# A Perceiver block on one core: the cross attention's opening takes its PSUM banks in turn, and the key-bias constant is made ahead of the second half of turned Wk

## The chip, the cores and the metric

The kernel runs on one core of a Trainium2 chip. The metric is the device time of one execution in microseconds (us). TensorE is PE in the profile, its weight loads are PEld, VectorE is DVE, ScalarE is ACT, GpSimd is POOL and SyncE, which issues the loads here, is SP.

## The reference, cut to what matters

A transformer block of three parts: cross attention of 64 x 64 rows of x on 64 contexts of 256 rows, self attention, and a mixture of experts. The change is in the first.

```python
def _L0_xattn_ref(query, key, value, Wq, bq, Wk, bk, Wv, bv, Wo, bo, ln_gamma, ln_beta):
    q = (query @ Wq + bq).reshape(b, sq, N_HEAD, KEY_DIM)         # 16 heads of 64
    k = (key @ Wk + bk).reshape(b, key.shape[1], N_HEAD, KEY_DIM)
    v = (value @ Wv + bv).reshape(b, value.shape[1], N_HEAD, VALUE_DIM)
    scores = jnp.einsum('bqhd,bkhd->bhqk', q, k) / TEMP
    attn = jax.nn.softmax(scores, axis=-1)
    out = jnp.einsum('bhqk,bkhd->bqhd', attn, v).reshape(b, sq, N_HEAD * VALUE_DIM)
    out = out @ Wo + bo + residual
    ...
x = x + _L0_xattn_ref(_layernorm(x, axis=-1), ctx_1024, ctx_1024, ...)
x = x + _L0_attn_ref(_layernorm(x, axis=-1), ...)
x = x + _L0_ffn_ref(_layernorm(x, axis=-1), ...)
```

## The kernel before

**Work.** Cross attention goes over the 64 batches in 16 groups of four. The keys are not projected. Instead each head's q is multiplied with its turned Wk (`do_fold`, one "fold" for each of eight heads of a half), and the result `qk` meets the transposed context `ctxT` in the scores. Every fp32 operand is split into an upper part, written by ACT out of PSUM (`ctxT_hi`, `qk_hi`, `wk_hi`), and a lower part, written by DVE as the PSUM value less the upper (`ctxT_lo`, `qk_lo`, `wk_lo`, L653). A product is then three matmuls (`exact3`, L930) or two (L973). So every result in PSUM goes PE, ACT, DVE, and only after DVE is its bank free.

**Steps.** A group has eight steps s: half = s // 4 picks the heads, b = s % 4 the batch. A step's chain is `do_scores` (24 matmuls into one of two score buffers), `peaks` on DVE (a maximum over the scores L690, then `top` L693 and `nbias` L695, which also read `qbk`), `exps` on ACT (L562), the division by the sum (`normalise`, on DVE in steps 0 and 7, on POOL in steps 1 to 6), and in the next step the transposes of the probabilities (`do_pT`, L1003, eight of them in two banks) and `do_pc` (with the context). scores(s), peaks(s), exps(s) and pT(s) stand below for these in step s of group 0; pT(1) is made of the probabilities of scores(0).

**The opening.** What comes before the loop is written as group -1 (first q for heads 0 to 7, their folds and all four `ctxT`) and group 0, which besides its own work turns the second half of Wk (`do_wkT`, L918, four pieces "wk") in steps 0 and 1 and makes the key-bias constant `qbk0` in step 0. The constant is q times bk for each row and head: POOL multiplies Wq by bk and adds up over each head (`weights_by_bk`, L460 and L466, result `wqb`), PE multiplies the normalised x by `wqb` (`do_qbk`, 12 small matmuls), and DVE keeps it (`keep_qbk`, L714). peaks(0) needs it. POOL then splits the contexts of group 0 (`split_ctx`, L437 and L439), which only `do_pc` reads.

**Banks.** Four PSUM banks are a ring (`ring`) for everything but the scores. Which item uses which bank is a table: `PAIR_BANKS` and `SINGLE_BANKS`, read by `ring_bank`. `ring_order` lists the items in the order in which they are used. `bank_for` lets PE wait until DVE or ACT has freed the item that had the bank before; semaphores `freed0` to `freed3` count this. The table is the same for every group. In group -1 it gives: xT 3, q 1 and 2, ctxT(0) 1, folds 0 to 7 the banks 1, 3, 0, 1, 2, 0, 3, 2, and ctxT(1) to ctxT(3) all bank 2. In group 0 it gives wk 0 to 3 the banks 0 to 3 and qbk0 bank 2; pT(1) uses banks 2 and 3.

**Order.** Every engine runs its instructions in the order in which its function (`tensor`, `vector`, `scalar`, `gpsimd`, `sync`) writes them. No scheduler moves anything.

Of the kernel before, what the change touches and what calls it, by code (L numbers as in the profile page):

```python
# [19 lines left out]
ALU = mybir.AluOpType  # L20
# [4 lines left out]
DC = D // P  # L25
# [5 lines left out]
DK = 64  # L31
# [9 lines left out]
RING = 4  # L41
# [77 lines left out]
def ring_order(kind):  # L119
# [10 lines left out]
    for s in range(STEPS):  # L130
        half, b = divmod(s, GB)
        if kind == 0 and s < 2:
            out += [("wk", 2 * s), ("wk", 2 * s + 1)]
        if kind == 0 and s == 0:
            out.append(("qbk0",))
        if half == 1 and g.next:
# [32 lines left out]
}  # L169
SINGLE_BANKS = {"ctxT": (1, 2, 2, 2), "o": (3, 0), "wk": (0, 1, 2, 3), "xT": (3,), "qbk": (1,), "qbk0": (2,)}  # L170


def ring_bank(key):

    if key[:2] in PAIR_BANKS and len(key) == 3:
        return PAIR_BANKS[key[:2]][key[2]]
    return SINGLE_BANKS[key[0]][key[1] if len(key) > 1 else 0]


def cross_attention(nc, ctx, t, x1_dram, ident, early, late, scores_banks, ring, following):  # L180
# [100 lines left out]

    bank_turns = [Turns(lambda kind, k=k: [key for key in ring_order(kind) if ring_bank(key) == k], -1, GROUPS)
                  for k in range(RING)]
# [5 lines left out]
    def place(g, key, groups_on=0):  # L289


        k = ring_bank(key)
        if isinstance(g.at, int):
            c, f = bank_turns[k].index(g.at + groups_on, key)
        else:
            c, f = bank_turns[k].index(g.at, key)
            c += bank_turns[k].loop * groups_on
        return k, (c + 1, f)
# [120 lines left out]
    def gpsimd(pool):  # L419
# [37 lines left out]

        def weights_by_bk(c):

            nc.gpsimd.tensor_tensor(products[:, 0], wq_raw[:, c, :], biases[:, 0], ALU.mult).then_inc(wqb_step, 1)  # L460
            pool.wait_ge(wqb_step, WQB_STEPS * c + 1)
            n = DK // 2
            parts = products[:, 0].rearrange("p (h d) -> p h d", d=DK)
            for i in range(WQB_STEPS - 1):
                out = parts[:, :, 0:n] if n > 1 else wqb[:, c, :].unsqueeze(2)
                nc.gpsimd.tensor_tensor(out, parts[:, :, 0:n], parts[:, :, n:2 * n], ALU.add).then_inc(wqb_step, 1)  # L466
                pool.wait_ge(wqb_step, WQB_STEPS * c + i + 2)
                n //= 2

        for g in turns(pool):  # L470
            if g.kind == -1:
                rsqrt(g, 0, ln_stats, ln_rstd, 1)
                pool.wait_ge(wq_in[0], 16)
                pool.wait_ge(wq_in[1], 16)
                pool.wait_ge(bk_in, 16)
                for c in range(DC):
                    weights_by_bk(c)
                nc.gpsimd.tensor_copy(wqb_hi[:, :, :], wqb[:, 0:DC, :]).then_inc(wqb_step, 1)
                pool.wait_ge(wqb_step, WQB_STEPS * DC + 1)
                nc.gpsimd.tensor_tensor(wqb_lo[:, :, :], wqb[:, 0:DC, :], wqb_hi[:, :, :],  # L480
# [153 lines left out]
    def vector(dve):  # L634
# [143 lines left out]
        for g in turns(dve):  # L778
# [40 lines left out]
            for s in range(STEPS):  # L819
                half, b = divmod(s, GB)  # L820
                if s == 0 and g.kind == 0:

                    for i in range(2):
                        wk_lower(g, i)
                    dve.wait_ge(wqb_done, 1)
# [6 lines left out]
                if g.cur:  # L832
                    peaks(g, s)
                if g.kind == 0 and s == 1:
                    for i in range(2, 4):
                        wk_lower(g, i)
# [74 lines left out]
    def tensor(pe):  # L911
# [161 lines left out]
        for g in turns(pe):  # L1073
# [1640 lines left out]
```

## Time and profile before

| | |
|---|---|
| three runs | 2158.69, 2160.35, 2160.77 us; median 2160.35 us |
| the profiled execution | 2161.38 us, of which its span is 2159.6 us |
| PE busy | 2099.8 us (97% of the span) |
| DVE, ACT, POOL busy | 1568.7 us (73%), 1269.5 us (59%), 941.1 us (44%) |
| mean granted clock of TensorE | 0.991 of full speed |
| share of PE in the chain that ended last | 75% |

The profiled execution is 1.03 us over the median, and what lies outside its span is 1.78 us. The views used below are: the chain of work that ended last, in order of time; the timeline, engine by engine; busy time and granted clock by stretch; and the issues of the loads with their time to landing. A bracket at the end of a timeline row gives the idle time of the engine before it and what ended it.

### The profile page before, as it was taken

To read this page: it belongs to the slowest core of one execution; us is meant where nothing else is said; L and a number is where in the kernel's file an instruction comes from. 1 tells how busy PE (TensorE), PEld (TensorE's weight loads), DVE (VectorE), ACT (ScalarE), POOL (GpSimd) and SP (SyncE) were. 2 spreads that over 40 slices of the span, in tenths; PEclk is the share of its full clock that TensorE was granted. 3 is DMA by queue.
4 is the path that set the end of the run, shared out by engine and by line. 5 is a ranking of instruction groups with operands and counts; after the bars stand their busy time and mean duration, and the time that the engine had idled before them with its cause. 6 is when DMAs were issued, how large, how long until landed. Compare 5 with 4: busy or idle time off the path is not lost.

```text
span 2159.6 us, 46904 instructions
## 1 busy us (share of the span) xinstructions
PE 2099.8 (97%) x15864; PEld 1853.6 (86%) x15865; DVE 1568.7 (73%) x2774; ACT 1269.5 (59%) x3067; POOL 941.1 (44%) x786
## 2 busy tenths in 40 slices
PE   7999999999999999999999999899998999999997
PEld 6889899888988898898998888678886888888886
DVE  5667767777677677677677776699996877666665
ACT  4656666665666666556666656467775335555553
POOL 3322332333233224223323332278884334777775
PEclk9999999999999999999999999999999999999999
DMA  5000010010000000100100100145442222333332
GB/s 154 6 25 22 13 34 19 15 34 15 19 24 24 19 24 10 34 22 12 34 19 15 34 10 1 48 157 167 156 129 94 88 79 55 56 53 53 53 54 42
DMA packets 100685, 103.90 MB, mean 48 GB/s; under 512 B 11952, under 2 KB 90160, under 8 KB 100624
## 3 DMA queue, kind: packets, MB, share of 16 engines
q1 hardware_dynamic: 86992, 84.47, 12.5%
q0 software_dynamic: 13632, 18.62, 5.4%
q8 instruction: 37, 0.61, 0.1%
q14 instruction: 24, 0.20, 0.0%
HBM read 72.52 MB, written 30.54 MB: 48 GB/s over the span
## 4 chain that ended last, share of the span: by engine, by line
PE 75%; POOL 9%; issue 6%; DVE 5%; ACT 2%; DMA 2%; POOLq 0%; SPq 0%; DVEq 0%; ACTq 0%
PE banks L930 38%; PE banks L973 6%; PE banks L1003 5%; PE banks L1031 5%; PE banks L1018 5%; POOL out_dram L2431 4%; PE banks L1672 3%; POOL r_x L2395 3%; PE banks L2270 2%; POOL index L2402 2%; DMA out_dram<-r_y,index 1%; PE banks L960 1%; PE banks L1735 1%; PE banks L1694 1%; PE banks L1751 1%
## 5 line engine op out<-in xcount | busy, mean ns | idle before, releaser
L930 PE MATMUL banks<-ctxT_hi,qk_hi 128*128 128x256 f32 x1024 | 301.5, 294 | 0.0
L930 PE MATMUL banks<-ctxT_hi,qk_lo 128*128 128x256 f32 x1024 | 290.1, 283 | 0.0
L930 PE MATMUL banks<-ctxT_lo,qk_hi 128*128 128x256 f32 x1024 | 288.2, 281 | 0.0
L562 ACT ACTIVATE probs<-banks,nbias 128x256 f32<-128x256 f32 x512 | 236.3, 486 | 81.1 <-DVE nbias L695 80.7
L451 POOL TENSOR_TENSOR rinv<-rsum,inverse 128x4 f32<-128x4 f32 x96 | 96.7, 1007 | 410.9 <-ACT probs L562 410.9
L569 ACT ACTIVATE pc<-banks 128x512 f32<-128x512 f32 x256 | 153.0, 598 | 190.4 <-PE banks L930 187.2
L653 DVE TENSOR_TENSOR qk_lo<-banks,qk_hi 128x512 fp32r<-128x512 f32 x256 | 163.7, 686 | 88.4 <-ACT qk_hi L524 88.3
L690 DVE TENSOR_REDUCE peak<-banks 128x4 f32<-128x1024 f32 x128 | 156.4, 1222 | 81.6 <-PE banks L930 81.6
L653 DVE TENSOR_TENSOR pT_lo<-banks,pT_hi 128x512 fp32r<-128x512 f32 x256 | 164.7, 685 | 58.2 <-ACT pT_hi L524 57.7
L930 PE MATMUL banks<-pT_hi,ctx_hi 128*128 128x512 f32 x512 | 204.7, 400 | 1.7 <-DVE pT_lo L653 1.7
L930 PE MATMUL banks<-pT_hi,ctx_lo 128*128 128x512 f32 x512 | 201.6, 394 | 0.0
L930 PE MATMUL banks<-pT_lo,ctx_hi 128*128 128x512 f32 x512 | 200.8, 392 | 0.0
L930 PEld LDWEIGHTS banks<-ctxT_lo,qk_hi 128*128 128x128 f32 x1024 | 196.1, 191 | 0.0
L930 PEld LDWEIGHTS banks<-ctxT_hi,qk_hi 128*128 128x128 f32 x1024 | 194.1, 190 | 0.6
L930 PEld LDWEIGHTS banks<-ctxT_hi,qk_lo 128*128 128x128 f32 x1024 | 193.0, 188 | 0.0
L454 POOL TENSOR_TENSOR probs<-probs,rinv 128x1024 f32<-128x1024 f32 x96 | 181.8, 1893 | 17.5 <-POOL rinv L451 17.5
L524 ACT ACTIVATE qk_hi<-banks 128x512 fp32r<-128x512 f32 x256 | 137.6, 601 | 77.8 <-PE banks L973 77.7
L437 POOL CAST ctx_hi<-ctx_raw 128x512 fp32r<-128x512 f32 x64 | 39.0, 610 | 299.6 <-PE banks L930 287.4
L673 DVE SCALAR_TENSOR_TENSOR q_st<-banks,bq_low,q_st 64x256 fp32r<-64x256 f32 x256 | 112.5, 479 | 55.3 <-ACT q_st L546 53.3
L1003 PE MATMUL banks<-ident,probs 128*128 128x128 f32 x1024 | 136.0, 275 | 7.3 <-DVE wk_lo L653 3.3
L524 ACT ACTIVATE pT_hi<-banks 128x512 fp32r<-128x512 f32 x256 | 139.8, 601 | 5.0 <-PE banks L1003 3.9
L973 PE MATMUL banks<-q_st,wk_hi 128*128 128x256 f32 x512 | 135.7, 299 | 5.5 <-DVE ctxT_lo L653 3.1
(271 smaller groups left out, 6161.0 us busy)
## 6 DMA issues: line engine op xcount, KB each, us to landing
ctx_raw<-in_ctx_dram SPq DMA_DIRECT2D x64, 256.0 KB, 2.7
experts_w<-in_L_ffn_We_dram SPq DMA_DIRECT2D x24, 512.0 KB, 3.9
x_in<-in_x_dram SPq DMA_DIRECT2D x16, 256.0 KB, 2.8
x_again<-in_x_dram SPq DMA_DIRECT2D x16, 256.0 KB, 2.8
x_stream<-z SPq DMA_DIRECT2D x16, 256.0 KB, 2.1
s_x<-x_stream SPq DMA_DIRECT2D x32, 128.0 KB, 3.7
s_x_again<-x_stream SPq DMA_DIRECT2D x32, 128.0 KB, 3.2
x_normalised<-s_xl SPq DMA_DIRECT2D x32, 128.0 KB, 1.7
```

Source lines behind the costliest of these rows:

```text
L454: nc.gpsimd.tensor_tensor(probs[:, s % 2], probs[:, s % 2], rinv[:, s % 2, :].unsqueeze(2).broadcast_to([P, PAIRS, SK]), ALU.mult).then_in ...
L524: nc.scalar.activation(out, bank, ACT.Identity).then_inc(hi_done, 1)
L562: nc.scalar.activation(probs[:, s % 2, p, :], scores[:, s % 2, p // 2, (p % 2) * SK:(p % 2 + 1) * SK], ACT.Exp, bias=nbias[:, s % 2, p:p + ...
L569: nc.scalar.activation(pc[:, c, :, at], bank.rearrange("p (h q) -> p h q", h=HALF), ACT.Identity).then_inc(free, 1)
L653: nc.vector.tensor_tensor(out, rows(ring[:, k, :]), hi, ALU.subtract).then_inc(freed[k], 1)
L673: last = nc.vector.scalar_tensor_tensor(out=q_st[DK:P, h, :], in0=ring[DK * hp:DK * hp + DK, k, i * GT:(i + 1) * GT], scalar=bq_low[:, tar ...
L690: link(nc.vector.tensor_reduce(peak[:, s % 2, :], scores[:, s % 2, :, :].rearrange("p j (i k) -> p (j i) k", i=2), AX_X, ALU.max))
L930: last = nc.tensor.matmul(out, a, b, start=(n == 0), stop=(n == 3 * len(pairs) - 1))
L973: last = nc.tensor.matmul(bank[:, c * GT:(c + 1) * GT], w[:, target * HALF + h, c * P:(c + 1) * P], q_st[:, h, :], start=(n == 0), stop=(n ...
L1003: last = nc.tensor.transpose(bank[:, p * P:(p + 1) * P], probs[:, (s - 1) % 2, p, k * P:(k + 1) * P], ident[:, :])
L1018: last = nc.tensor.matmul(bank[hp * DK:(hp + 1) * DK, i * GT:(i + 1) * GT], wv[:, c, col:col + DK], pc[:, c, h, :], start=(c == 0), stop=( ...
L1031: last = nc.tensor.matmul(bank[:, n * D:(n + 1) * D], oT[:, m, n * P:(n + 1) * P], wo[:, m, :], start=(m == first), stop=(m == first + PAI ...
```

## The change

1. In group -1 the bank of an item is its place in `ring_order`, modulo 4: xT 0, q 1 and 2, ctxT(0) 3, folds 0 to 7 the banks 0, 1, 2, 3, 0, 1, 2, 3, and ctxT(1), (2), (3) the banks 0, 1, 2. All other groups keep the table.
2. In group 0, wk 0 to 3 take the banks 0, 1, 0, 1 and qbk0 takes bank 3.
3. In step 0 PE does `do_qbk` ahead of `do_wkT` 0 and 1, and DVE does `keep_qbk` and `peaks` ahead of `wk_lower` 0 and 1.
4. POOL makes `wqb` in two halves of the heads, the first of which waits only for the first half of Wq: four chunks of 512 columns where there were two of 1024, each of seven operations.

```diff
     for s in range(STEPS):
         half, b = divmod(s, GB)
+        if kind == 0 and s == 0:
+            out.append(("qbk0",))
         if kind == 0 and s < 2:
             out += [("wk", 2 * s), ("wk", 2 * s + 1)]
-        if kind == 0 and s == 0:
-            out.append(("qbk0",))
...
-SINGLE_BANKS = {"ctxT": (1, 2, 2, 2), "o": (3, 0), "wk": (0, 1, 2, 3), "xT": (3,), "qbk": (1,), "qbk0": (2,)}
+SINGLE_BANKS = {"ctxT": (1, 2, 2, 2), "o": (3, 0), "wk": (0, 1, 0, 1), "xT": (3,), "qbk": (1,), "qbk0": (3,)}
-def ring_bank(key):
+def ring_bank(key, kind):
+    if kind == -1:
+        return ring_order(kind).index(key) % RING
...
-        def weights_by_bk(c):
-            nc.gpsimd.tensor_tensor(products[:, 0], wq_raw[:, c, :], biases[:, 0], ALU.mult).then_inc(wqb_step, 1)
+        def weights_by_bk(half, c):
+            done = WQB_STEPS * (DC * half + c)
+            cols = slice(half * HALF * DK, (half + 1) * HALF * DK)
+            nc.gpsimd.tensor_tensor(products[:, 0, cols], wq_raw[:, c, cols], biases[:, 0, cols],
+                                    ALU.mult).then_inc(wqb_step, 1)
...
-                pool.wait_ge(wq_in[0], 16)
-                pool.wait_ge(wq_in[1], 16)
                 pool.wait_ge(bk_in, 16)
-                for c in range(DC):
-                    weights_by_bk(c)
+                for half in range(2):
+                    pool.wait_ge(wq_in[half], 16)
+                    for c in range(DC):
+                        weights_by_bk(half, c)
...
                 if s == 0 and g.kind == 0:
-                    for i in range(2):
-                        wk_lower(g, i)
                     dve.wait_ge(wqb_done, 1)
                     keep_qbk(g, ("qbk0",))
...
                 if g.cur:
                     peaks(g, s)
-                if g.kind == 0 and s == 1:
-                    for i in range(2, 4):
+                if g.kind == 0 and s < 2:
+                    for i in range(2 * s, 2 * s + 2):
                         wk_lower(g, i)
...
                 if g.cur:
                     do_scores(g, s)
+                if g.kind == 0 and s == 0:
+                    pe.wait_ge(wqb_done, 1)
+                    do_qbk(g, ("qbk0",))
                 if g.kind == 0 and s < 2:
                     for i in range(2 * s, 2 * s + 2):
                         do_wkT(g, i)
-                if g.kind == 0 and s == 0:
-                    pe.wait_ge(wqb_done, 1)
-                    do_qbk(g, ("qbk0",))
```

**PE in group -1**, before: the first matmul of ctxT(0), of fold 0, 4, 5 and 7, and the three ctxT after the folds, with the semaphores that each waits for (in the rows, `banks` is PSUM and `pc` the room in which the raw weights lie).

```order
L960 MATMUL banks<-ident,ctx_raw 128x128 [waits freed1,ctx_in0]
L973 MATMUL banks<-q_st,wk_hi 128x256 [waits freed1,setup_lo]
L973 MATMUL banks<-q_st,wk_hi 128x256 [waits freed2,setup_lo]
L973 MATMUL banks<-q_st,wk_hi 128x256 [waits freed0]
L973 MATMUL banks<-q_st,wk_hi 128x256 [waits freed2]
L960 MATMUL banks<-ident,ctx_raw 128x128 [waits freed2,ctx_in1]
L960 MATMUL banks<-ident,ctx_raw 128x128 [waits freed2,ctx_in2]
L960 MATMUL banks<-ident,ctx_raw 128x128 [waits freed2,ctx_in3]
```

The same matmuls in the changed kernel:

```order
L963 MATMUL banks<-ident,ctx_raw 128x128 [waits ctx_in0]
L976 MATMUL banks<-q_st,wk_hi 128x256 [waits freed1,setup_lo]
L976 MATMUL banks<-q_st,wk_hi 128x256 [waits freed0,setup_lo]
L976 MATMUL banks<-q_st,wk_hi 128x256 [waits freed1]
L976 MATMUL banks<-q_st,wk_hi 128x256 [waits freed3]
L963 MATMUL banks<-ident,ctx_raw 128x128 [waits freed0,ctx_in1]
L963 MATMUL banks<-ident,ctx_raw 128x128 [waits freed1,ctx_in2]
L963 MATMUL banks<-ident,ctx_raw 128x128 [waits freed2,ctx_in3]
```

ctxT(0) no longer waits for a bank. Fold 0 waited on bank 1 for ctxT(0) itself, and now waits on bank 1 only for the first q. The last three ctxT wait on three banks instead of on one.

**DVE in step 0 of group 0**, before, from the lower part of Wq's second half on:

```order
L647 TENSOR_TENSOR wq_lo<-pc,wq_hi 128x2x512 [waits wq_hi_done]
L653 TENSOR_TENSOR wk_lo<-banks,wk_hi 128x512 [waits hi_done] x2
L714 SCALAR_TENSOR_TENSOR qbk<-banks,wqb 64x2x8 [waits filled2,wqb_done]
L690 TENSOR_REDUCE peak<-banks 128x4 [waits scores_done,small_in,freed2]
L693 SCALAR_TENSOR_TENSOR top<-peak,qbk 128x4 [waits dve_step]
L695 TENSOR_TENSOR nbias<-qbk,top 128x4 [waits dve_step]
L725 RECIPROCAL rinv<-rsum 128x4 [waits exp_done]
```

The same in the changed kernel:

```order
L652 TENSOR_TENSOR wq_lo<-pc,wq_hi 128x2x512 [waits wq_hi_done]
L719 SCALAR_TENSOR_TENSOR qbk<-banks,wqb 64x2x8 [waits filled3,wqb_done]
L695 TENSOR_REDUCE peak<-banks 128x4 [waits scores_done,small_in,freed3]
L698 SCALAR_TENSOR_TENSOR top<-peak,qbk 128x4 [waits dve_step]
L700 TENSOR_TENSOR nbias<-qbk,top 128x4 [waits dve_step]
L658 TENSOR_TENSOR wk_lo<-banks,wk_hi 128x512 [waits hi_done] x2
L730 RECIPROCAL rinv<-rsum 128x4 [waits exp_done]
```

The two `wk_lo` moved from ahead of the constant to behind `nbias`, which ACT waits for.

**PE in steps 0 and 1 of group 0**, before: wk 0 and 1 (their first transposes), the constant, wk 2 and 3, and pT(1) in its two banks.

```order
L918 MATMUL banks<-ident,pc 64x128 [waits wk_in1]
L930 MATMUL banks<-wqb_hi,xT_hi 128x16 [waits freed2,wqb_done]
L918 MATMUL banks<-ident,pc 64x128 [waits freed2,wk_in1]
L1003 MATMUL banks<-ident,probs 128x128 [waits freed2,probs_done]
L1003 MATMUL banks<-ident,probs 128x128 [waits freed3]
```

The same in the changed kernel, where the constant comes first:

```order
L933 MATMUL banks<-wqb_hi,xT_hi 128x16 [waits wqb_done]
L921 MATMUL banks<-ident,pc 64x128 [waits freed0,wk_in1]
L921 MATMUL banks<-ident,pc 64x128 [waits freed1,wk_in1]
L1006 MATMUL banks<-ident,probs 128x128 [waits freed2,probs_done]
L1006 MATMUL banks<-ident,probs 128x128 [waits freed3]
```

Before, pT(1) waited in banks 2 and 3 for the `wk_lo` of wk 2 and 3; now those banks were last used by ctxT(3) and by the constant, and it is wk 2 and 3 that wait, for wk 0 and 1.

## Rows read from the trace of the kernel before

**Rows 1.** By stretch: length, busy PE, PEld, DVE, ACT, POOL, clock, DMA share, GB/s.

```profile
80.00:1100.00 1020.00, 1018.67 (x7190) 912.46 (x7190) 739.17 (x1346) 626.45 (x1661) 320.10 (x267) 1.00 0.07 22
```

**Rows 2.** Chain that ended last, in order of time: start, us, what.

```profile
21.16 3.58 PE banks L973 x16
...
34.33 4.77 PE banks L930 x24
...
39.10 1.90 PE banks L918 x32
...
41.00 1.45 PE banks L930 x12
...
51.80 2.89 PE banks L930 x24
```

**Rows 3.** Timeline of PE: start, us, what, then idle before and releaser.

```profile
31.11 0.63 PE L960 MATMUL banks<-ident,ctx_raw 128*128 128x128 f32 x4 [1.50 <-DVE ctxT_lo L653]
...
33.98 0.56 PE L930 MATMUL banks<-ctxT_hi,qk_hi 128*128 128x256 f32 x1
...
50.64 1.16 PE L1003 MATMUL banks<-ident,probs 128*128 128x128 f32 x8 [3.34 <-DVE wk_lo L653]
```

**Rows 4.** Timeline of DVE and ACT in the folds.

```profile
15.52 3.58 DVE L673 SCALAR_TENSOR_TENSOR q_st<-banks,bq_low,q_st 64x256 fp32r<-64x256 f32 x8
...
20.33 0.68 DVE L653 TENSOR_TENSOR ctxT_lo<-banks,ctxT_hi 128x512 fp32r<-128x512 f32 x1
...
24.76 2.31 ACT L524 ACTIVATE qk_hi<-banks 128x512 fp32r<-128x512 f32 x4 [0.33 <-PE banks L973]
...
25.39 2.51 DVE L653 TENSOR_TENSOR qk_lo<-banks,qk_hi 128x512 fp32r<-128x512 f32 x4 [0.24 <-ACT qk_hi L524]
```

**Rows 5.** By stretch, PE alone: length, busy (matmuls), granted clock, DMA share, GB/s.

```profile
22.00:23.00 1.00, 1.00 (x7) 0.50 0.97 389
```

**Rows 6.** Timeline of DVE and ACT from the constant to the second wk_lo.

```profile
42.55 0.73 DVE L714 SCALAR_TENSOR_TENSOR qbk<-banks,wqb 64x16 f32<-64x16 f32 x4 [0.18 <-PE banks L930]
...
43.31 1.23 DVE L690 TENSOR_REDUCE peak<-banks 128x4 f32<-128x1024 f32 x1
...
44.97 0.47 ACT L562 ACTIVATE probs<-banks,nbias 128x256 f32<-128x256 f32 x1 [3.32 <-DVE nbias L695]
...
47.14 1.22 DVE L726 TENSOR_TENSOR probs<-probs,rinv 128x1024 f32<-128x1024 f32 x1
...
49.81 1.28 DVE L653 TENSOR_TENSOR wk_lo<-banks,wk_hi 128x512 fp32r<-128x512 f32 x2
```

**Rows 7.** Timeline of POOL: products of wqb, its end, last context split.

```profile
14.03 2.43 POOL L460 TENSOR_TENSOR probs<-pc,oT 128x1024 f32<-128x1024 f32 x1 [8.19 <-DMA pc<-in_L_xattn_Wq_dram]
...
26.68 0.25 POOL L480 TENSOR_TENSOR wqb_lo<-wqb,wqb_hi 128x32 fp32r<-128x32 f32 x1
...
33.27 1.27 POOL L439 TENSOR_TENSOR ctx_lo<-ctx_raw,ctx_hi 128x512 fp32r<-128x512 f32 x1
```

**Rows 8.** Issues of two loads on SP's queue, and their time to landing in us.

```profile
2.32 0.47 SPq L370 DMA_DIRECT2D oT<-in_L_xattn_bk_dram  x1
...
17.00 0.53 SPq L389 DMA_DIRECT2D wo<-in_L_xattn_Wo_dram  x1
...
oT<-in_L_xattn_bk_dram SPq DMA_DIRECT2D x1, 512.0 KB, 7.3
...
wo<-in_L_xattn_Wo_dram SPq DMA_DIRECT2D x1, 1024.0 KB, 11.9
```

**Rows 9.** Timelines of POOL and DVE where the two meet.

```profile
55.65 1.89 POOL L454 TENSOR_TENSOR probs<-probs,rinv 128x1024 f32<-128x1024 f32 x1 [0.18 <-POOL rinv L451]
...
55.97 1.59 DVE L693 SCALAR_TENSOR_TENSOR top<-peak,qbk 128x4 f32<-128x4 f32 x1
...
141.02 0.61 POOL L437 CAST ctx_hi<-ctx_raw 128x512 fp32r<-128x512 f32 x1
...
141.13 0.52 DVE L695 TENSOR_TENSOR nbias<-qbk,top 128x4 f32<-128x4 f32 x1
```

More of the change, by code:

```diff
@@ L280, in cross_attention @@
     pool_past = sem("pool_past")
-    bank_turns = [Turns(lambda kind, k=k: [key for key in ring_order(kind) if ring_bank(key) == k], -1, GROUPS)
+    bank_turns = [Turns(lambda kind, k=k: [key for key in ring_order(kind) if ring_bank(key, kind) == k], -1, GROUPS)
                   for k in range(RING)]
@@ L289, in place @@
     def place(g, key, groups_on=0):
-        k = ring_bank(key)
+        k = ring_bank(key, g.at + groups_on if isinstance(g.at, int) else g.kind)
         if isinstance(g.at, int):
@@ L456, in normalise @@
                                     ALU.mult).then_inc(probs_pool, 1)
-        def weights_by_bk(c):
-            nc.gpsimd.tensor_tensor(products[:, 0], wq_raw[:, c, :], biases[:, 0], ALU.mult).then_inc(wqb_step, 1)
-            pool.wait_ge(wqb_step, WQB_STEPS * c + 1)
+        def weights_by_bk(half, c):
[3 more added lines that the diff above has]
+                                    ALU.mult).then_inc(wqb_step, 1)
+            pool.wait_ge(wqb_step, done + 1)
             n = DK // 2
-            parts = products[:, 0].rearrange("p (h d) -> p h d", d=DK)
+            parts = products[:, 0, cols].rearrange("p (h d) -> p h d", d=DK)
             for i in range(WQB_STEPS - 1):
-                out = parts[:, :, 0:n] if n > 1 else wqb[:, c, :].unsqueeze(2)
+                out = parts[:, :, 0:n] if n > 1 else wqb[:, c, half * HALF:(half + 1) * HALF].unsqueeze(2)
                 nc.gpsimd.tensor_tensor(out, parts[:, :, 0:n], parts[:, :, n:2 * n], ALU.add).then_inc(wqb_step, 1)
-                pool.wait_ge(wqb_step, WQB_STEPS * c + i + 2)
+                pool.wait_ge(wqb_step, done + i + 2)
                 n //= 2
@@ L472, in gpsimd @@
                 rsqrt(g, 0, ln_stats, ln_rstd, 1)
-                pool.wait_ge(wq_in[0], 16)
-                pool.wait_ge(wq_in[1], 16)
                 pool.wait_ge(bk_in, 16)
-                for c in range(DC):
-                    weights_by_bk(c)
+                for half in range(2):
+                    pool.wait_ge(wq_in[half], 16)
+                    for c in range(DC):
+                        weights_by_bk(half, c)
                 nc.gpsimd.tensor_copy(wqb_hi[:, :, :], wqb[:, 0:DC, :]).then_inc(wqb_step, 1)
-                pool.wait_ge(wqb_step, WQB_STEPS * DC + 1)
+                pool.wait_ge(wqb_step, WQB_STEPS * DC * 2 + 1)
                 nc.gpsimd.tensor_tensor(wqb_lo[:, :, :], wqb[:, 0:DC, :], wqb_hi[:, :, :],
```

## The prediction

> **What bounds the kernel now.** First read the share of PE in the chain that ended last, in the small table: 75%. Then the busy time by stretch [rows 1]: from 80 to 1100 us PE is busy for 1018.67 of 1020 us at the full clock. Once the loop runs there is no gap that could swallow or return time, and the change leaves every instruction of the loop and every bank in it alone. So the change is worth what it moves the start of the loop, one for one, and all of it has to be read in the first 62 us.
>
> There the chain in order of time [rows 2] and the timelines [rows 3, 4, 6] show four things to look for.
>
> (a) PE starts fold 0 at 21.16 us, right after DVE's ctxT_lo of 20.33 [rows 2, 4], since ctxT(0) had fold 0's bank.
>
> (b) After the folds, ctxT(1) to ctxT(3) go through one bank. Each has to be made by PE, split by ACT, lowered by DVE, and only then comes the next: PE starts one at 31.11 us after 1.50 us of idling for DVE's ctxT_lo of the one before it [rows 3]. scores(0) starts only at 33.98.
>
> (c) PE, which had idled, runs at half clock: the 24 matmuls of scores(0) cost 4.77 us on the chain and the 24 of scores(2) 2.89 [rows 2]. The stretch 22 to 23 us has a granted clock of 0.50, that is 1.2 of 2.4 GHz, after PE's idle time up to 21.16 [rows 2, 5].
>
> (d) From the end of scores(0), 39.10, the exps(0) on ACT are waited for until 44.97, and pT(1) comes at 50.64, after 3.34 us of idling, released by wk_lo [rows 2, 3, 6].
>
> **Banks in turn, group -1.** No instruction is added or removed. ctxT(0) finds bank 3 empty, so it follows the turned Wk at once, and fold 0 waits only for the first four heads of q: DVE is half through its 3.58 us of q_st at 15.52 + 1.8 = 17.3 [rows 4]. Folds 0 to 3 then fit in four banks. From fold 4 on a bank is needed again, and DVE is what frees it: it ends ctxT_lo at 20.33 + 0.68 = 21.0 as before, and then finds four results waiting. It lowers one every 0.63 us (four in 2.51), ACT's four take 2.31, so DVE sets the pace [rows 4]. Fold 6's lower half is then done at 21.0 + 7 x 0.63 = 25.4, which frees bank 2 for ctxT(3); with its 0.63 us on PE [rows 3] scores(0) starts at **26.0 instead of 33.98: 8.0 us**. The three ctxT_lo lie behind the folds on DVE and end near 27.8; only scores(1) and later need them.
>
> **The clock in scores(0).** In my replay PE has folds and transposes from 21.8 to 26 with gaps of under half a microsecond, while before it had 1.50 us of idling ahead of each ctxT. I take the full clock, 2.89 instead of 4.77 us. scores(0) then ends at 26.0 + 3.0 = **29.0 instead of 39.10: 10.1 us by now**. Bounds: nothing (clock as before, 1.9 us lost), or the full clock; the value next to it is scores(2).
>
> **The constant first.** Before, wk 0 and 1 (1.90 us) and the 12 small matmuls (1.45) lay between scores(0) and DVE's qbk [rows 2]; now only the 1.45. From the end of the constant on PE, 42.45, to the exps(0), 44.97, are 2.52 us: qbk 0.73, the maximum 1.23, top, nbias [rows 6]. So exps(0) could start at 29.0 + 1.45 + 2.5 = 33.0. On ACT wk_hi 0 and 1 stand ahead of it: PE ends wk 1 at 30.45 + 1.90 = 32.4, and at 0.6 us for one upper half ACT is free at 33.0 too. That edit gains 1.9 us and has no more to give.
>
> **What peaks(0) now meets.** At 26 to 34 us POOL works. Rows show what that does: POOL's operation from 55.65 took 1.89, and DVE's top of 128x4, started at 55.97, took 1.59, up to POOL's end; a nbias started at 141.13 took 0.52 under a CAST that had started at 141.02 and ran 0.61 [rows 9]. top and nbias read SBUF twice. The maximum, qbk and the lower halves read PSUM. POOL's last context split ended at 33.27 + 1.27 = 34.5 before [rows 7], ten microseconds before peaks(0). Now top comes at 29.0 + 1.45 + 0.1 + 0.73 + 1.23 = 32.5. POOL starts its products when bk has landed, 2.32 + 7.3 = 9.6 [rows 8], not at 14.03; before, the stretch took 26.93 - 14.03 = 12.9 us [rows 7], and it now has 14 operations more at 0.15 to 0.3 us of fixed cost each (a tiny one takes 0.25), about 3.5. wqb is ready at 26 to 27 (needed on PE at 29.0, so hidden by 2 us; before it was ready 14 us early, so this edit gains nothing), and the splits, 7.6 us, end at 33.7 to 35. So top and nbias each can wait for an operation of 0.61 or 1.27 us: 0 to 2.5 us in all, and I take **1.2**: exps(0) at 34.2.
>
> The Trainium skill, page "SBUF — State Buffer", section "Who interferes with whom", puts it as a rule: a DVE instruction with two SBUF inputs and a GpSimd instruction that reads SBUF exclude each other, and whoever issues second is fully blocked. By that rule, which the rows above agree with, the wait in peaks(0) is a part of the sum and not an accident. Without it the sum would be 0.4 us better, as the next part shows.
>
> **From exps(0) to pT(1).** wk_lo 0 and 1 (1.28) moved behind nbias; exps(0) hide them (2.17 us until the multiplication starts). Probabilities are ready 2.17 + 1.22 = 3.4 us after exps(0) start [rows 6], at 37.6. PE has by then done, without a gap: 29.0 + 1.45 + 1.90 (wk 0, 1) + 2.89 (scores(1)) + 1.90 (wk 2, 3, whose banks wk_lo 0 and 1 free at 34.9 and 35.6) = 37.2. So pT(1) comes at 37.6, and at 37.2 if the ports cost nothing: the first 0.8 us of a port wait cost 0.4. Before, pT(1) also waited for DVE's maximum over scores(1) and wk_lo, 48.36 to 50.5; now banks 2 and 3 are long free. **50.64 becomes 37.6: 13.0 us.** Behind it nothing is later by more: nbias(1) is ready 1.45 us after the multiplication [rows 6], at 39.1, as ACT ends pT_hi; scores(2), q and pc follow pT(1) as before. The end of the group, the loads for group 1 (issued before 40 us, read after 68) and the loop shift along.
>
> **Sum.** 2161.38 - 13.0 = 2148.4 for an execution like the profiled one, which lay 1.03 over the median: **2147.4 us**.
>
> **Rivals.**
> 1. *The clock stays low in scores(0), or falls in the folds.* PE does idle from about 19.4 to 21.8, and an idle stretch of 3 us had brought the half clock at 21 [rows 2, 5]. scores(0) costs 1.9 more, the folds up to 0.7: 2149.3 to 2150.0.
> 2. *The port costs more.* DVE's product of the two biases (two SBUF inputs, at 13.0, two operations ahead of the q_st of 15.52) now stands against POOL, which began only at 14.03. One POOL operation ahead of it is up to 1.27 us (a split's) and goes straight into q_st and the folds; with the full 2.5 us in peaks(0), of which 1.7 pass: 3.0 instead of the 0.4 that the sum has, 2150.0.
> 3. *A better turn in step 2.* In peaks(2) top lost 1.4 us to POOL [rows 9]. If the exps(1) end only 0.4 us later against scores(2) than they did, top and nbias get ahead of POOL: 2146.0.
> 4. *Slower: DVE finds no gap at all.* If the biases' product doesn't get in between two POOL operations, it waits until POOL's first pause, after the splits, at 33.7 or later instead of 13.0. All of DVE's queue, q_st first, is 20.7 us late, less 13.0: 2168.0. It decides from 26.0 on. Against it: nbias at 141.13 ended at 141.65, between POOL's CAST and its next operation [rows 9].
> 5. *The gain is eaten by something that doesn't shift.* peaks(0) also wait for the small loads, the last of which, wo, lands at 17.00 + 11.9 = 28.9 [rows 8]; needed at 31.3, so 2.4 us are in hand, and each later microsecond costs one. Or the new order doesn't show at all, because another wait had been just behind the banks. Half eaten would be 2154, all of it 2160.
>
> **Numbers.** Forecast 0.62, rival 1 0.16, rival 2 0.08, rival 3 0.06, rival 4 0.03, rival 5 0.05 (0.02 half, 0.03 more). The range reaches from rival 3 less the spread of the runs to rivals 1 and 2 and a microsecond: 2144.8 to 2151.2, and leaves out 0.12 or so with the edges. A measurement can tell 0.2%, 4.3 us, from no change: faster 0.93 (all but 4 and most of 5), the same 0.03, slower 0.04.
>
> **What the profile after would show.** scores(0) starts near 26.0, and its 24 matmuls take 2.9 us at clock 1.00 (rival 1: 4.8 at 0.50); no PE idling for ctxT_lo ahead of ctxT(2) and (3) over 0.5 us; exps(0) at 33 to 34.3, with top or nbias longer than 0.2 us and ending with a POOL operation (rival 2: the biases' product over 1.3 us); pT(1) at 37.2 to 37.6, released by the probabilities; wqb_lo done by 27; and from 62 us on the old trace, 13 us earlier. Wrong it would be if scores(0) starts after 28, if the biases' product lasts past 15, or if steps 1 to 4 of group 0 are longer than before by more than a microsecond.

## The result, and the profile after

The changed kernel takes 2147.5 us (median of four runs, 2144.19 to 2149.09), the one before 2160.56 (2158.69 to 2161.27). The ratio is 0.9938, with a 95% interval of 0.9926 to 0.995: 13.1 us faster. 2147.4 was forecast, in a range of 2144.8 to 2151.2. The profiled execution took 2147.61 us, its span is 2145.9, so 13.7 less than the span before.

The page of the changed kernel, its span and the row of TensorE. PE is busy for as long as before within 2.7 us, so that of the 13.7 us that the span lost about 11 are idle time of PE.

```profile
span 2145.9 us, 46808 instructions
...
PE 2097.1 (98%) x15864; PEld 1850.5 (86%) x15865; DVE 1568.1 (73%) x2774; ACT 1271.4 (59%) x3067; POOL 946.7 (44%) x800
```

The chain that ended last, over the stretch that changed (start, us, what):

```profile
20.07 0.61 DVE ctxT_lo L658
...
20.73 4.33 PE banks L976 x20
...
25.06 1.39 PE banks L963 x12
...
26.45 4.12 PE banks L933 x36
...
30.56 1.90 PE banks L921 x32
...
35.53 1.90 PE banks L921 x32
...
37.42 1.02 PE banks L1006 x8
...
41.36 1.24 DVE peak L695
...
42.62 1.65 DVE top L698
```

From 20.73 to 41.3 us the chain is PE alone (the pieces left out are PE's too): 20 matmuls of the folds, the twelve transposes of the last three contexts in one go (1.39 us where the profile before had 2.13 us for each four, [rows 3]), scores(0) with the constant (4.12 us for 36 matmuls), wk, scores(1), wk, pT(1), scores(2). The waits of DVE, of ACT and of DVE and POOL for each other are off it. Then peaks(2) comes with top at 1.65 us, as before [rows 9].

PE's timeline at the starts of scores(0) and pT(1), which answer to [rows 3], and the busy time with the granted clock for two stretches (stretch, length, PE busy, clock, DMA share, GB/s), which answer to [rows 5]:

```profile
26.20 0.36 PE L933 MATMUL banks<-ctxT_hi,qk_hi 128*128 128x256 f32 x1
...
37.36 1.09 PE L1006 MATMUL banks<-ident,probs 128*128 128x128 f32 x8
...
22.00:24.00 2.00, 2.00 (x11) 0.50 1.04 391
...
27.00:28.00 1.00, 1.00 (x11) 1.00 0.06 19
```

scores(0) starts at 26.20 (before 33.98) at the full clock, pT(1) at 37.36 (before 50.64) and without a wait. In the folds the clock was at half, 1.2 of 2.4 GHz.

DVE, ACT and POOL around peaks(0), which answer to [rows 6, 7]:

```profile
31.44 1.22 DVE L695 TENSOR_REDUCE peak<-banks 128x4 f32<-128x1024 f32 x1
...
32.70 0.28 DVE L698 SCALAR_TENSOR_TENSOR top<-peak,qbk 128x4 f32<-128x4 f32 x1
...
33.02 0.52 DVE L700 TENSOR_TENSOR nbias<-qbk,top 128x4 f32<-128x4 f32 x1
...
33.57 0.47 ACT L567 ACTIVATE probs<-banks,nbias 128x256 f32<-128x256 f32 x1 [0.46 <-DVE nbias L700]
...
31.68 1.28 POOL L441 TENSOR_TENSOR ctx_lo<-ctx_raw,ctx_hi 128x512 fp32r<-128x512 f32 x1
...
32.91 0.61 POOL L439 CAST ctx_hi<-ctx_raw 128x512 fp32r<-128x512 f32 x1
```

top ran until 32.98, when POOL's ctx_lo ended at 32.96, and nbias until 33.54, when the CAST ended at 33.52. The two cost 0.48 us over their 0.16 each. Another DVE instruction with two SBUF inputs met POOL before them: the lower half of Wq's second half took 1.64 us, where the kernel before had 1.23, and the ctx_lo that POOL started behind it took 2.13 instead of 1.27:

```profile
28.28 1.64 DVE L652 TENSOR_TENSOR wq_lo<-pc,wq_hi 128x1024 fp32r<-128x1024 f32 x1
...
28.92 2.13 POOL L441 TENSOR_TENSOR ctx_lo<-ctx_raw,ctx_hi 128x512 fp32r<-128x512 f32 x1
```

Neither is on the chain. exps(0) start at 33.57, before at 44.97.

How the shift goes on, from the first stores of a finished group on SP's queue: the first is issued at 193.10 us before and at 179.96 now (13.14 earlier), the one of the fourteenth group at 1284.48 and 1270.66 (13.82). Nothing takes the gain back.

### The profile page after: what moved, and what is told of

It is laid out like the page before. It is cut to its first block, busy times and chain, and to the rows that moved or that the text cites. A ratio compares the mean times of both kernels' runs of the same rounds, so it can differ in the third digit from the quotient of the medians.

```text
span 2145.9 us, 46808 instructions
## 1 busy us (share of the span) xinstructions
PE 2097.1 (98%) x15864; PEld 1850.5 (86%) x15865; DVE 1568.1 (73%) x2774; ACT 1271.4 (59%) x3067; POOL 946.7 (44%) x800
## 4 chain that ended last, share of the span: by engine, by line
PE 76%; POOL 10%; issue 6%; DVE 4%; ACT 2%; DMA 2%; POOLq 0%; DVEq 0%; ACTq 0%
PE banks L933 38%; PE banks L976 6%; PE banks L1006 5%; PE banks L1021 5%; PE banks L1034 5%; POOL out_dram L2434 4%; PE banks L1675 3%; POOL r_x L2398 3%; PE banks L2273 2%; POOL index L2405 2%; DMA out_dram<-r_y,index 2%; PE banks L1738 1%; PE banks L963 1%; PE banks L1697 1%; PE banks L1754 1%
```

## The experiments

The profiled executions don't all start alike: DVE's q_st begins between 13.2 and 16.7 us, with almost the same code ahead of it. So the traces are compared from the start of q_st on (the last experiments are about that start). There is one trace for each kernel. The changed kernel itself was measured in four runs only, apart from the experiments and at another time, and they reach from 2144.19 to 2149.09: a difference of 1 to 3 us between its median and an experiment's is not shown by the medians. What a trace shows of a single wait is. The table is worked out from the start times in each trace: scores(0), exps(0) and pT(1) less the start of q_st, and exps(2) less pT(1). In the rows marked * the product of the biases stands behind q_st instead of ahead of it, so their q_st doesn't compare with that of the other rows.

| kernel | median, us | q_st | scores(0) | exps(0) | pT(1) | exps(2) - pT(1) |
|---|---|---|---|---|---|---|
| before | 2160.1 to 2161.4 | 15.52 | +18.46 | +29.45 | +35.12 | 7.16 |
| changed | 2147.5 | 15.18 | +11.02 | +18.39 | +22.18 | 7.13 |
| banks only | 2150.82 | 14.90 | +11.09 | +21.08 | +26.75 | 8.36 |
| constant only | 2157.1 | 16.27 | +19.30 | +28.19 | +32.46 | 7.13 |
| ctxT in one bank | 2151.02 | 13.29 | +15.28 | +23.66 | +27.93 | 7.13 |
| whole products | 2146.81 | 16.65 | +10.20 | +17.13 | +21.36 | 7.12 |
| multiplication held | 2144.38 | 13.37 | +11.10 | +18.29 | +22.64 | 5.65 |
| splits held | 2144.71 | 15.66 | +10.21 | +17.64 | +21.90 | 5.65 |
| product late * | 2147.96 | 16.01 | +10.20 | +18.34 | +21.80 | 7.13 |
| both * | 2143.85 | 15.74 | +10.21 | +18.49 | +21.95 | 6.56 |
| longer start | 2146.15 | 13.96 | +10.21 | +18.29 | +22.65 | 7.13 |
| longer start, held | 2144.5 | 13.17 | +10.21 | +17.95 | +22.33 | 5.65 |
| before, held | 2160.38 | 13.61 | +18.92 | +29.46 | +35.13 | 7.22 |

### Banks alone (e1_banks_only)

```diff
+def ring_bank(key, kind):
+    if kind == -1:
+        return ring_order(kind).index(key) % RING
```

The rest is the kernel before, `qbk0`, `wk` and POOL included.

> The kernel before with edit 1 alone (banks in turn in group -1). My theory: the parts add up, and this one brings what it moves the start of scores(0): scores(0) at 26.2 us as in the changed kernel, at the full clock, over at 29.2; then wk 0 and 1 (1.9 us) and the constant (1.4), qbk on DVE at 32.6, exps(0) at 35.1, and pT(1) 5.7 us behind that, at 40.8, released by wk_lo, against 50.64 before and 37.36 changed: 9.9 us faster than before, 2150.7 us. Rival: the two edits need each other (once the banks turn, the old order of the constant is hidden anyway), and pT(1) comes within 1 us of the changed kernel's: 2147.5 to 2148.5 us.

Measured: 2150.82 us (2149.39 to 2151.28), ratio 0.9952 (0.9935 to 0.997). In the profiled execution scores(0) are as early as in the changed kernel, exps(0), counted from q_st, 1.2 us later than expected, and here is why (timelines of DVE and POOL):

```profile
34.58 1.18 DVE L695 SCALAR_TENSOR_TENSOR top<-peak,qbk 128x4 f32<-128x4 f32 x1
...
34.45 1.28 POOL L441 TENSOR_TENSOR ctx_lo<-ctx_raw,ctx_hi 128x512 fp32r<-128x512 f32 x1
...
41.65 1.94 PE L1005 MATMUL banks<-ident,probs 128*128 128x128 f32 x8 [4.34 <-DVE wk_lo L655]
```

top took 1.18 us instead of 0.16, until ctx_lo, which POOL had started 0.13 us before it, ended at 35.73. pT(1) then came 5.67 us after exps(0), as before the change, and had to wait for wk_lo. After the 4.34 us of idling PE came back at half clock (pT(1) took 1.94 us instead of 1.09, scores(2) 4.75 instead of 2.89), and exps(2) follow 8.36 us behind though top in peaks(2) takes 0.16. The rival (the order of the constant is hidden) is out: pT(1) is 4.6 us later than in the changed kernel.

### The constant alone (e2_constant_only)

```diff
-SINGLE_BANKS = {... "wk": (0, 1, 2, 3), ... "qbk0": (2,)}
+SINGLE_BANKS = {... "wk": (0, 1, 0, 1), ... "qbk0": (3,)}
-                    for i in range(2):
-                        wk_lower(g, i)
                     dve.wait_ge(wqb_done, 1)
...
+                if g.kind == 0 and s == 0:
+                    pe.wait_ge(wqb_done, 1)
+                    do_qbk(g, ("qbk0",))
```

> The kernel before with edits 2 and 3 alone (banks of wk and qbk0; constant and maxima ahead of turned Wk), group -1 and POOL as before. My theory: scores(0) starts at 34.0 us and runs at half clock as before, ends at 39.1; exps(0) at 43.1, pT(1) bound by PE at 47.3 and no longer released by wk_lo, against 50.64: 3.3 us faster than before, 2157.2 us, so that this and the banks alone add up to the whole, 13.2. Rival: the constant's order is worth only the 1.9 us to exps(0) (the wait for wk_lo comes back in another bank), 2158.6 us.

Measured: 2157.1 us (ten runs, 2152.76 to 2158.45), ratio 0.9984 (0.9974 to 0.9993): 3.0 us. From scores(0) to pT(1) are 13.16 us (32.46 - 19.30) where before there were 16.66: 3.5 us. As expected, pT(1) no longer waits: PE has no idle time ahead of it. The two edits apart give 9.3 and 3.0 us by their medians, 12.3 together, and the whole 13.1. From the start of q_st to the end of the profiled executions it is 9.6 and 3.7 us, 13.3 together, and the whole 13.4. Within the scatter they add up.

### ctxT in one bank (e4_ctxT_one_bank)

```diff
     if kind == -1:
-        return ring_order(kind).index(key) % RING
+        return 2 if key[0] == "ctxT" and key[1] > 0 else ring_order(kind).index(key) % RING
```

> The changed kernel with ctxT(1) to ctxT(3) in bank 2 again, folds in turn. My theory: the three go through PE, ACT and DVE one after the other, 2.13 us each, from 25.8 us on: scores(0) starts at 30.8 instead of 26.20. PE idles 1.5 us ahead of each, as before the change; if that is what had brought the half clock, the 24 matmuls of scores(0) take 4.8 instead of 2.9 us too: 4.6 to 6.5 us slower than the changed kernel, 2152 to 2154. Rival: the clock in scores(0) has nothing to do with the waits for one bank, and only the 4.6 us show, with clock 1.00. Second rival: the folds were the main part and the single bank costs under 2 us, since DVE is busy with the folds anyway.

Measured: 2151.02 us (2148.99 to 2151.36). PE's timeline, and its clock in scores(0):

```profile
25.24 1.09 PE L963 MATMUL banks<-ident,ctx_raw 128*128 128x128 f32 x4 [1.50 <-DVE ctxT_lo L658]
...
27.83 1.09 PE L963 MATMUL banks<-ident,ctx_raw 128*128 128x128 f32 x4 [1.50 <-DVE ctxT_lo L658]
...
28.00:30.00 2.00, 2.00 (x11) 0.50 0.34 46
...
30.00:32.00 2.00, 2.00 (x11) 0.50 0.57 138
```

The wait of 1.50 us for DVE is back word for word as in [rows 3], scores(0) start 4.3 us later against q_st, and they run at clock 0.50 for most of their length. pT(1) is 5.75 us later in the profiled execution (27.93 - 22.18), within the 4.6 to 6.5 expected, the median only 3.5; this run's q_st began 1.9 us early. Its folds ran at the full clock, those of the changed kernel at half, which cost that one 0.8 us: against kernels with full folds (splits held, whole products) pT(1) is 6.0 to 6.6 us later. So of some 9 to 10 us that the banks bring, 3.5 (medians) to 6.6 (traces) are the one bank of the contexts and the half clock behind it, and the rest, by difference, is the folds. The rival without the clock is out: in all four kernels in which the three contexts share bank 2 (before, constant only, this one, before with the held multiplication) scores(0) start at clock 0.50, and in none of the other nine.

### Whole products on POOL (e3_whole_products)

The changed kernel with `weights_by_bk(c)` in its old form, over 1024 columns and behind both halves of Wq.

> The changed kernel with POOL's products of Wq and bk in their old form, two chunks of 1024 columns that wait for both halves of Wq (edit 4 undone). My theory: POOL begins at 14.0, wqb is ready at 26.9 against 29.2 when PE asks for it, the splits end at 34.5, and the time is the changed kernel's within a microsecond, 2147.5: edit 4 brings nothing. DVE's product of the biases is 1.22 us either way. Rival: the halves matter, since the constant is now asked for early: PE idles ahead of it, or top and nbias of peaks(0) wait longer for POOL, over 1 us in all, 2148.5 or more.

Measured: 2146.81 us (2146.54 to 2147.54) against 2147.5 of the changed kernel: edit 4 brings nothing that is seen, and costs nothing that is seen. The trace is a mild test, though, since this execution started latest of all (q_st at 16.65): wqb was ready at 28.1 and asked for at 29.8. In the trace with the longer start below, where scores(0) came earliest but one, PE waited 0.60 us for wqb even with the halves. What did happen at the place that rivals 2 and 4 feared, the product of the biases on DVE against POOL, stands in the changed kernel's timelines:

```profile
12.67 1.22 DVE L707 SCALAR_TENSOR_TENSOR probs<-oT 128x1024 f32<-128x1024 f32 x1
...
12.87 2.16 POOL L464 TENSOR_TENSOR probs<-pc,oT 128x512 f32<-128x512 f32 x1
```

DVE's product started 0.2 us earlier and took its usual 1.22 us; it was POOL's that grew, from 1.27 (the other three chunks) to 2.16.

### POOL's multiplication held behind peaks(2) (e5_mult_after_peaks2)

```diff
             pool.wait_ge(rinv_done, len(POOL_STEPS) * g.at + s)
+            if g.kind == 0 and s == 1:
+                pool.wait_ge(peak_done, 3)
```

> The changed kernel, with POOL's multiplication of the probabilities in step 1 of group 0 held back until DVE has done nbias of peaks(2). My theory: DVE's top in peaks(2), 1.64 us long in the changed kernel, only waits for that POOL operation. Here it takes 0.16, exps(2) start at 43.1 instead of 44.49, POOL's operation runs 43.1 to 45.0 and is still hidden (pT(2) came at 49 and 50), and the loop starts 1.4 us earlier: 2146.1 us. Rival: top is long for a reason of its own (or DVE then meets another POOL operation), exps(2) stay at 44.5, or pT(2) waits for the late multiplication: no gain, 2147.5.

Measured: 2144.38 us (2143.66 to 2147.26), ratio 0.9927 (0.9914 to 0.9941).

```profile
33.84 2.12 DVE L733 TENSOR_TENSOR probs<-probs,rinv 128x1024 f32<-128x1024 f32 x1
...
41.27 0.16 DVE L700 SCALAR_TENSOR_TENSOR top<-peak,qbk 128x4 f32<-128x4 f32 x1
...
33.61 1.27 POOL L441 TENSOR_TENSOR ctx_lo<-ctx_raw,ctx_hi 128x512 fp32r<-128x512 f32 x1
...
41.80 1.89 POOL L458 TENSOR_TENSOR probs<-probs,rinv 128x1024 f32<-128x1024 f32 x1 [0.98 <-DVE nbias L702]
```

top takes 0.16 us, and the exps(2) follow pT(1) by 5.65 instead of 7.13 us: the 1.5 us that top lost were POOL's. The median is 3.1 us lower, twice that; the other half is likely scatter. The profiled execution also had an early start (q_st at 13.37); from q_st to its end it is 2.1 us shorter than the changed kernel's. The first rows show another meeting: the multiplication of DVE's own normalise(0), two SBUF inputs, began at 33.84 behind POOL's ctx_lo of 33.61 and took 2.12 us instead of 1.22. Of these 0.9 us pT(1) saw a part: PE idled 0.32 us for the probabilities, and pT(1) came 11.54 us behind scores(0) instead of 11.16.

### Splits held behind peaks(0) (e6_splits_after_peaks0)

```diff
+                pool.wait_ge(peak_done, 1)
                 for b in range(GB):
                     split_ctx(g, b)
```

> The changed kernel, with POOL's context splits of group 0 held back until DVE has done nbias of peaks(0). My theory: top and nbias of peaks(0) take 0.16 us each instead of 0.28 and 0.52, exps(0) start at 33.1 instead of 33.57, and nothing comes of it, since pT(1) is bound by PE's own queue at 37.36. The splits then run from 33 to 41 and meet DVE's multiplication (two SBUF inputs, at 35.3) and top and nbias of peaks(1) (at 37.7), each of which can wait for up to 1.3 us: 0 to 1.5 us slower than the changed kernel, 2147.5 to 2149. Rival: exps(0) set pT(1), and the 0.5 us are gained: 2147.0, with pT(1) at 36.9.

Measured: 2144.71 us (2143.48 to 2146.67). No gain or a loss was expected, and the median is 2.8 us lower (1.8 us from q_st to the end of the profiled execution). Up to peaks(1) the waits moved as the theory has it:

```profile
32.90 0.16 DVE L699 SCALAR_TENSOR_TENSOR top<-peak,qbk 128x4 f32<-128x4 f32 x1
...
35.47 1.61 DVE L732 TENSOR_TENSOR probs<-probs,rinv 128x1024 f32<-128x1024 f32 x1
...
38.25 0.54 DVE L699 SCALAR_TENSOR_TENSOR top<-peak,qbk 128x4 f32<-128x4 f32 x1
...
42.82 0.16 DVE L699 SCALAR_TENSOR_TENSOR top<-peak,qbk 128x4 f32<-128x4 f32 x1
...
36.09 2.13 POOL L441 TENSOR_TENSOR ctx_lo<-ctx_raw,ctx_hi 128x512 fp32r<-128x512 f32 x1
...
43.27 1.90 POOL L456 TENSOR_TENSOR probs<-probs,rinv 128x1024 f32<-128x1024 f32 x1 [0.18 <-POOL rinv L453]
```

In peaks(0) top is free. The multiplication of normalise(0) took 1.61 and top of peaks(1) 0.54, with 0.4 us lost each. pT(1) came without a wait of PE ahead of it: +21.90, less than the changed kernel's +22.18 only because scores(0) came 0.8 us earlier (its folds ran at the full clock), and 11.69 us behind scores(0) against 11.16 there; 0.28 us of it is a wait of PE for wqb, whose last operation took 1.32 us instead of 0.25 under DVE's wq_lo. But POOL was so late with its splits that its multiplication of step 1 began at 43.27, after top of peaks(2) had run at 42.82 for 0.16 us. That is the turn that the third rival of the prediction had in mind, made by an edit: 5.65 us from pT(1) to exps(2). The expectation had been worked out only up to peaks(1).

### The product of the biases behind the folds (e7_product_late, e8_both)

```diff
-                biases_product()
                 dve.wait_ge(bq_in, 32)
...
                 for b in range(1, GB):
                     ctx_lower(g, b)
-                wq_lower(1)
+                biases_product()
```

`wq_lower(1)` moved to behind wk_lo 2 and 3. The second kernel has the held multiplication too.

> The changed kernel, with DVE's product of the two biases (2.5 us for two instructions) moved from ahead of q_st to behind the last ctxT_lo of group -1, and the lower half of Wq's second half moved to behind wk_lo 2 and 3. My theory: DVE sets the pace of the opening, so q_st, wk_lo, ctxT_lo and the folds come 1.2 us earlier, scores(0) start at 25.0, pT(1) at 36.2 as long as the product is done before the constant (27.0 to 29.5, up to 30.8 if it meets POOL's splits): 0.4 to 1.2 us faster than the changed kernel, 2146.3 to 2147.1. Rival: ACT's q_st or the half clock in the folds is as late as DVE, and the start of scores(0) moves by under 0.4 us: 2147.5, or later because the product delays peaks(0).

> The edits of the two kernels before this last one in one (POOL's multiplication of step 1 behind peaks(2); product of the biases behind the folds). My theory: both gains pass to the loop, 1.4 and 0.4 to 1.2 us: 2144.9 to 2145.7. Rival: they take from the same idle time of PE in step 2 and only 1.4 us remain, 2146.1, or the measured median does not tell them from the changed kernel's, whose runs spread from 2144.2 to 2149.1.

Measured: 2147.96 us (2145.39 to 2148.18) and 2143.85 us (2142.79 to 2144.34), ratio 0.9919 (0.9906 to 0.9933). The medians show no gain of the move by itself. The trace shows where its rivals were right (timeline of DVE):

```profile
16.01 3.57 DVE L678 SCALAR_TENSOR_TENSOR q_st<-banks,bq_low,q_st 64x256 fp32r<-64x256 f32 x8 [1.96 <-ACT q_st L551]
...
28.00 2.00 DVE L707 SCALAR_TENSOR_TENSOR probs<-oT 128x1024 f32<-128x1024 f32 x1
...
30.03 1.22 DVE L709 TENSOR_REDUCE wqb<-probs 128x16 f32<-128x1024 f32 x1
...
33.80 0.52 DVE L700 TENSOR_TENSOR nbias<-qbk,top 128x4 f32<-128x4 f32 x1
```

DVE, without the product, waited 1.96 us for ACT's q_st. This execution started late, and in the whole products kernel, which also did, DVE with the product was only 0.15 us further behind ACT (q_st on DVE 1.10 us after q_st on ACT began, here 0.95). In the other traces it is 1.4 to 2.3 us, so some of the 1.2 us that the edit was to bring may be there in other executions; no trace shows it. Behind the folds the product met POOL's splits (2.00 us instead of 1.22), qbk followed only at 31.28, and exps(0) came 8.14 us after scores(0) instead of 7.37. And the moved wq_lo (1.2 us) now stands in DVE's queue ahead of peaks(2): with the held multiplication top takes 0.16 us there, and yet exps(2) follow pT(1) by 6.56 us and not by 5.65. With the held multiplication it is the fastest kernel of the study by its median, 0.5 us ahead of the held multiplication alone. Their runs overlap, so which of the two is better is open.

### A longer start (e9_warm22, e10_warm22_mult)

```diff
-WARM = 18
+WARM = 22
```

> The changed kernel with 22 instead of 18 transposes of the identity on PE at its very start, so that PE works until 6.7 us, when the first transposes of x are ready, and not to 5.95. It is about what the traces so far left open: the profiled runs of one and the same opening differ by up to 2 us before q_st starts on DVE (13.3 to 16.7 us), and in the two earliest of them the first 32 transposes of Wk took 1.97 us, in the others 2.9 to 3.7. My theory: in the others PE is still at its low rate there, and a longer start makes the full rate come in time more often: the 32 transposes take 1.97 us, q_st starts about 1.6 us earlier than the 15.18 of the changed kernel, and the median is 1 to 1.6 us lower, 2146. Rival: four transposes more don't change when the rate rises, or they delay the transposes of x: the 32 transposes stay at 3 us or more in the profiled run and the median is 2147.5 or more.

> The same 22 transposes together with POOL's multiplication of step 1 held back behind peaks(2), as in the kernel that had measured 2144.4 us. My theory: the two are far apart in time and add up: 2143 us, with exps(2) 5.65 us behind pT(1). Rival: the longer start brings nothing, 2144.4.

Measured: 2146.15 us (2143.59 to 2146.57) and 2144.5 us (2141.27 to 2146.53). PE's first 32 transposes of Wk, in the changed kernel and with the longer start:

```profile
7.82 3.56 PE L921 MATMUL banks<-ident,pc 128*64 128x128 f32 x32
```

```profile
8.18 1.97 PE L921 MATMUL banks<-ident,pc 128*64 128x128 f32 x32 [0.60 <-DMA pc<-in_L_xattn_Wk_dram]
```

1.97 us instead of 3.56, and q_st began at 13.96 instead of 15.18. In both profiled runs with 22 transposes they took 1.97; with 18 it was so in three of eleven (the kernels with ctxT in one bank, with the held multiplication, and the one before with it), and in the other eight 2.88 to 3.68. But those eight are of two kinds. In five (before, changed, banks only, product late, both) the four transposes of x just ahead took 1.12 us, where the others have 0.66 to 0.83: there PE had not come to its full rate, as the theory says. In the other three (constant only, whole products, splits held) the transposes of x took 0.66, then PE idled 1.64 to 1.80 us for Wk to land, and the granted clock fell to 0.50. PE in the kernel with whole products, whose clock reads 0.50 from 9 to 14 us:

```profile
6.73 0.66 PE L1041 MATMUL banks<-ident,xln 128*128 128x128 f32 x4 [1.31 <-DVE xln L757]
...
9.18 3.68 PE L918 MATMUL banks<-ident,pc 128*64 128x128 f32 x32 [1.80 <-DMA pc<-in_L_xattn_Wk_dram]
```

In both traces with 22 transposes Wk landed early (PE waited for it 0.60 us at most), so whether a longer start helps when it lands late is open. The medians tell the gain less well still: 1.35 us better than the changed kernel as expected, and no better than the held multiplication alone (2144.5 against 2144.38). The mechanism is likely for the first kind, a gain in the median isn't shown.

### The kernel before, multiplication held (e11_before_mult)

> The kernel before with nothing but POOL's multiplication of step 1 held back behind peaks(2). My theory: the wait of top for POOL is a cost of its own that the change neither made nor mended: top takes 0.16 instead of 1.59 us, exps(2) start 5.7 us behind pT(1) instead of 7.16, and the loop starts 1.4 us earlier: 2159.0 to 2159.3 us against 2160.6. Rival: in the kernel before it was hidden by something else, and nothing is gained.

Measured: 2160.38 us (eleven runs, 2156.52 to 2162.5), ratio 0.9994 (0.9985 to 1.0003), 0.2 us. The profile shows top at 0.16 us, as the theory has it, and what ate it (timeline of DVE; chain that ended last):

```profile
55.57 0.16 DVE L695 SCALAR_TENSOR_TENSOR top<-peak,qbk 128x4 f32<-128x4 f32 x1
...
49.95 4.34 PE banks L932 x24
```

The 24 matmuls of scores(2) took 4.34 us where they had 2.89 [rows 2]: PE had idled 3.34 us ahead of pT(1) and came back at half clock (with the banks alone, after 4.34 us, they took 4.75). In the trace of the kernel before, the same 3.34 us were followed by the full clock, so this is not bound to happen. In the changed kernel PE doesn't idle there. So the same edit is worth 1.5 us in one kernel and nothing in this profiled run of the other. The medians don't settle it: 1.4 us, a ratio of 0.9994, lies inside the interval.

## Why the prediction was right, and where it was not

**What it rests on.** The loop shifts as a whole: shown by the stores, 13.14 us at the first and 13.82 at the fourteenth, with 13.0 forecast at pT(1).

**Banks in turn.** scores(0) at 26.20, forecast 26.0. Part of the agreement is luck: q_st began 0.34 us earlier than before, and counted from it the forecast was 10.5 us, the changed kernel had 11.02, and the kernels whose folds ran at the full clock 10.2. The way there was wrong in one step: "Folds 0 to 3 then fit in four banks". Banks 2 and 3 belong to the second q and to ctxT(0), and PE waits for both:

```profile
18.81 0.39 PE L976 MATMUL banks<-q_st,wk_hi 128*128 128x256 f32 x1 [0.52 <-DVE q_st L678]
...
20.73 0.38 PE L976 MATMUL banks<-q_st,wk_hi 128*128 128x256 f32 x1 [1.18 <-DVE ctxT_lo L658]
```

Fold 2 started at 18.81 behind q_st and fold 3 at 20.73 behind ctxT_lo. It cost next to nothing, because DVE, which sets the pace, only came to the first fold at 20.59. With the half clock from 21.4 on, PE's folds then took 0.85 us each, more than DVE's 0.63, and from 20.73 until scores(0) the chain is PE's and not DVE's.

**The clock in scores(0).** Full, as taken. The first rival came half true: the folds ran at half clock, priced at up to 0.7 us. Of the nine kernels with all banks in turn, the six in which they ran at the full clock have scores(0) 10.20 or 10.21 us behind q_st, the other three 11.02 to 11.10: 0.8 us. Which of the two comes isn't set by the code: the kernels with the held multiplication and with the splits held are the same up to there, and one had half, the other full. That PE's waits for one bank bring the half clock to scores(0) is shown by the kernel with ctxT in one bank.

**The constant first.** 3.0 us by itself. The sum took pT(1) at 37.6, released by the probabilities, and had PE ready at 37.2. It was PE's to set: 37.36, without a wait, with the probabilities ready at 36.97. The number is right because the two paths were worked out to within 0.4 us of each other; which of them would end last was not.

**The ports in peaks(0).** Taken at 1.2 us, measured 0.48; bounds 0 and 2.5. In the other kernels whose splits ran beside peaks(0) it was 0.04 (whole products) to 1.0 (banks alone): it depends on where in POOL's sequence DVE arrives. It didn't matter, since PE was behind anyway. The rule of the Trainium skill, page "SBUF — State Buffer", section "Who interferes with whom", that the second to issue is blocked until the first finishes, agrees with the pairs shown here, in both directions: 1.64 us of top under POOL, and 2.16 us of POOL's product under DVE's. The prediction had counted only one direction and only up to pT(1). Two were missing from its list of those in danger: the multiplication of normalise(0), which lost 0.9 us where the multiplication of step 1 was held, and wq_lo. It had written that the lower halves read PSUM; wq_lo reads SBUF twice, and took 1.64 us in the changed kernel and 2.30 with the whole products, where 1.23 is its time alone.

**Edit 4.** Nothing expected, nothing seen, in a trace that tests it little. wqb was ready at 26.3 (26 to 27 forecast), the splits ended at 34.9 (33.7 to 35).

**The fourth rival** had DVE find no gap between POOL's operations. DVE's product started at 12.67, as the last small operation of POOL's first chunk (12.59 to 12.79) ran out, and held up POOL's next product instead.

**The small differences.** The medians differ by 13.1 and the spans by 13.7, pT(1) by 13.28. The parts that don't repeat are each larger than the error of 0.1 us in the forecast: q_st 0.34 us earlier, the half clock in the folds, another half clock that fell on other work (62.4 to 65.8 us before, 58.9 to 62.3 now). That the number fits to a tenth is chance; that it fits within 1.5 us is not.

## What to carry to other kernels

Where a result has to go through three engines before its bank is free, items that follow each other in one bank cost the whole round trip each (here 2.13 us), and the idle time it leaves can cost PE its clock in the work behind (here 4.77 us for 24 matmuls instead of 2.89). Of a result that another engine waits for (here nbias) and work that nobody waits for yet (wk_lo), put the first ahead, and look up which bank each frees. When an edit brings DVE and POOL together in time, list every instruction of DVE with two SBUF inputs and every one of POOL that reads SBUF, not only the first, and in both directions.

## What the runs showed of the hardware that was not expected

The first 32 transposes of Wk took 1.97 us in some executions and up to 3.68 in others of nearly the same code. The column of the granted clock tells it only in part. In the three traces in which PE had idled for Wk it falls to 0.50. In the five in which the transposes of x had taken long already, it reads 1.00 from the start, against the times of the instructions (115 ns for a transpose of Wk with product late, 62 ns in the fast traces). So a 1.00 at the start of an execution has to be checked against the time of a known instruction. With Wk's landing (PE started on it at 7.4 to 9.2 us) this moves q_st by up to 3.5 us from one profiled execution to another. It may be a good part of the spread of the runs, 2157.45 to 2165.79 for the kernel before in fifteen runs; that isn't shown, since only one execution of a kernel has a trace.

The beat of the loop, the stores from the first to the fourteenth group divided by 13, is 83.95 or 83.96 us in the three kernels with the old banks in group -1 (before, constant only, before with the held multiplication) and 83.86 to 83.92 in the other ten, whose loop has the same instructions in the same banks. From the first to the fourteenth store that makes 0.4 to 1.3 us, and 0.7 us between the changed kernel and the one before. What carries it over is open: no run here tells it apart.
